# Inverse deviations on ScalarE, ranks behind the second transposition, and the first row loads from ScalarE's queue in a two-stage MetaFormer kernel

## The chip, the cores and the metric

One core of a Trainium2 chip. The time is the device time of one launch in microseconds (us), lower is better. "Profiled execution" is one run recorded by the hardware profiler; all rows and clock times below are of it, and its us count from the start of its span.

## The reference

The input `x` is 8 images of 64 channels and 16x16 pixels, so 2048 tokens of 64 channels.

```python
kq = w_kq @ xn + b_kq; v = w_v @ xn + b_v          # xn: layer norm of x over channels, eps 1e-6
ctx = softmax(kq.T @ kq) @ v                       # 256 x 256 per image
t = x + w_o @ ctx + b_o                            # a token is a row of 64
tn = layer_norm(t)                                 # eps 1e-5
probs = softmax(tn @ router_w.T)                   # 8 experts, the best 2 of each token
out = t + sum over the 2 chosen: gate * (silu(tn @ w1[e].T) * (tn @ w3[e].T)) @ w2[e].T   # 682 wide
```

All of it is fp32.

## The kernel before, in words

There is no scheduler: each engine runs its own hand-written instruction list, and semaphores tie the lists together. A wait holds back everything that stands behind it on its engine.

**Stage one** works on four pairs `p` of images, four tiles of 128 tokens each. Per pair, ScalarE normalises (`normalise`, L440), copies the transposed rows (`xT_copy`), the key-query product (`kq_copy`), the value product (`u_copy`) and the transposed weights (`probsT_copy`, L474), and takes `exponentials` (L466), two per pair. VectorE takes the row maxima (`row_max`), the sum of residual and attention (`residual`), the two best experts (`tops`, `choose`), and the moments of the new rows (`t_statistics`). TensorE's `rank(p)` counts, by matmuls of ones, how many tokens went to each expert before; from it VectorE makes the row number of each token (`positions`, L658 and L662), and `normalise_t` writes the normalised rows (`xrows`, L643). GpSimd scatters them to `xs` in HBM, sorted by expert: 8 indirect DMAs per pair, 32 in all (`scatter_row`, L374), one after the other. GpSimd also computes both inverse deviations, as variance plus epsilon to the power of -0.5 (`inverse_deviation`, `t_deviation`, L349 and L364), between its other work.

TensorE's list holds matmuls that compute nothing which is used (`fill`, `keep_busy`), between the others.

**Tables.** After pairs 0 and 1 (`KNOWN = (2, 3, 4)`), VectorE works out which expert each of the first 8 slots of 128 rows belongs to, and where its rows begin (`subtiles_of_experts`, `owners_of_slots`, `rows_of_slots`, L703). These are tables in SBUF; SyncE reads them into registers, one load per number (L298 the owner, L302 the row), and issues DMAs at those addresses: `load_weights(i)` four of 565 KB each per quad of slots (L294), `load_rows(i)` four of 32.5 KB (L310). Phase 1 opens slots 8 to 15 after pair 2, phase 2 slots 16 to 38 after pair 3. The row loads of a phase wait until its scatters have landed (`landed`).

**Stage two** has 39 slots in 10 quads. Per quad: VectorE doubles the loaded rows (`pair_up`, L791), TensorE turns them (`turn_x`, L1034), ScalarE copies them (`columns`, tile `x_cols`, L507). Then six steps of up projection (L1055, L1057), `silu` on ScalarE (L515), product on VectorE (`multiply`, tile `hid`, L836), and the down projection (L1082). `up(g)` waits for `multiply(g - 3)`, so TensorE can be three steps ahead of VectorE. VectorE's list puts `pair_up(i + 2)` ahead of the first `multiply` of quad `i + 1`, and puts table work between the multiplications of quads 0 and 1: `rows_of_slots(1)`, which ends with L714 and releases phase 1's loads, stands after the second product of quad 0, and the tables of phase 2 behind the last product of quad 1. GpSimd scatters the results to `ys` (L383). A last stage loads, weighs and adds them.

## Time and profile before

| | |
|---|---|
| median of 3 runs | 179.76 us (178.6 to 181.26) |
| profiled execution, its own time | 177.17 us |
| its span | 175.4 us |
| TensorE busy | 142.0 us (81%) |
| VectorE, GpSimd, ScalarE busy | 99.8, 85.8, 71.2 us |
| mean granted clock of TensorE | 0.942 of full speed |

The span is what the trace covers. Busy shares are means over stages with different limits, so they say little by themselves.

### The profile page before, as it was taken

To read this page: it belongs to the slowest core of one execution; us is meant where nothing else is said; L and a number is where in the kernel's file an instruction comes from. 1 tells how busy PE (TensorE), PEld (TensorE's weight loads), DVE (VectorE), ACT (ScalarE), POOL (GpSimd) and SP (SyncE) were. 2 spreads that over 40 slices of the span, in tenths; PEclk is the share of its full clock that TensorE was granted. 3 is DMA by queue.
4 is the path that set the end of the run, shared out by engine and by line. 5 is a ranking of instruction groups with operands and counts; after the bars stand their busy time and mean duration, and the time that the engine had idled before them with its cause. 6 is when DMAs were issued, how large, how long until landed. Compare 5 with 4: busy or idle time off the path is not lost.

```text
span 175.4 us, 4915 instructions
## 1 busy us (share of the span) xinstructions
PE 142.0 (81%) x1697; PEld 119.7 (68%) x1697; DVE 99.8 (57%) x372; ACT 71.2 (41%) x141; POOL 85.8 (49%) x114
## 2 busy tenths in 40 slices
PE   1489969590892596996699999999999999985672
PEld 1357746370561495895598999999999989874262
DVE  1626756858739857589357474637364736443050
ACT  2347664512430144262153545454545445443011
POOL 2695223877773772577653353525262626266000
PEclk9999999999579569999699999999999999999699
DMA  4999400001781692179697969596969881000345
GB/s 120 322 288 279 110 0 11 23 15 34 234 338 35 151 392 83 43 251 344 206 381 215 396 199 373 174 356 194 325 207 348 275 327 49 13 30 15 95 156 120
DMA packets 19893, 33.00 MB, mean 188 GB/s; under 512 B 7691, under 2 KB 13100, under 8 KB 19868
## 3 DMA queue, kind: packets, MB, share of 16 engines
q1 hardware_dynamic: 16732, 29.55, 52.1%
q0 software_dynamic: 2272, 2.35, 4.0%
q10 hardware_dynamic: 864, 0.79, 1.4%
q8 instruction: 14, 0.23, 0.6%
q14 instruction: 11, 0.09, 0.2%
HBM read 25.55 MB, written 7.13 MB: 186 GB/s over the span
## 4 chain that ended last, share of the span: by engine, by line
issue 31%; POOL 29%; PE 17%; DMA 8%; ACT 5%; DVE 5%; SPq 1%; POOLq 1%; ACTq 0%; DVEq 0%
POOL ys L383 20%; POOL xs L374 9%; PE psum L1055 4%; ACT probs L466 3%; DMA xs<-xrows,pos 2%; DMA y_in<-ys 2%; PE psum L1126 2%; PE psum L940 2%; PE psum L929 2%; PE psum L919 1%; DVE xrows L643 1%; DMA ys<-y_out,y_row 1%; DMA proj<-projections 1%; DMA x_in<-xs 1%; PE psum L1034 1%
## 5 line engine op out<-in xcount | busy, mean ns | idle before, releaser
L383 POOL DMA_INDIRECT ys<-y_out,y_row x39 | 37.7, 967 | 43.3 <-DVE y_out L848 34.1
L1055 PE MATMUL psum<-x_cols,weights 64*128 64x128 f32 x390 | 52.0, 288 | 3.5 <-DMA weights<-experts 3.3
L1055 PEld LDWEIGHTS psum<-x_cols,weights 64*128 64x128 f32 x390 | 48.1, 197 | 7.5 <-issue 5.4
L1057 PE MATMUL psum<-x_cols,weights 64*128 64x128 f32 x390 | 52.0, 288 | 0.0
L836 DVE TENSOR_TENSOR hid<-psum,act_sb 128x512 f32<-128x512 f32 (+1 forms) x50 | 33.7, 678 | 30.6 <-ACT act_sb L515 30.3
L1057 PEld LDWEIGHTS psum<-x_cols,weights 64*128 64x128 f32 x390 | 48.1, 197 | 0.0
L515 ACT ACTIVATE act_sb<-psum 128x512 f32<-128x512 f32 (+1 forms) x50 | 29.3, 586 | 29.8 <-PE psum L1055 29.8
L374 POOL DMA_INDIRECT xs<-xrows,pos x32 | 31.4, 980 | 18.4 <-DVE xrows L643 10.0
L1082 PE MATMUL psum<-hid,weights 128*64 128x128 f32 x468 | 28.8, 276 | 0.0
L1082 PEld LDWEIGHTS psum<-hid,weights 128*64 128x64 f32 x468 | 25.9, 137 | 1.8 <-DVE hid L836 0.3
L929 PE MATMUL psum<-ident,probs 128*128 128x128 f32 x32 | 6.6, 340 | 8.9 <-ACT probs L466 8.7
L929 PEld LDWEIGHTS psum<-ident,probs 128*128 128x128 f32 x32 | 4.2, 169 | 13.0 <-ACT probs L466 12.1
L528 ACT COPY y_cols<-psum 128x256 f32<-128x256 f32 (+1 forms) x10 | 3.6, 361 | 21.0 <-PE psum L1082 21.0
L507 ACT COPY x_cols<-psum 128x512 f32<-128x512 f32 (+1 forms) x10 | 5.7, 574 | 12.0 <-PE psum L1034 12.0
L1034 PE MATMUL psum<-ident,x_pairs 128*128 128x128 f32 x39 | 7.3, 316 | 3.0 <-DVE x_pairs L791 3.0
L940 PEld LDWEIGHTS psum<-u_sb,probsT 128*128 128x128 f32 x64 | 8.6, 209 | 1.0 <-issue 1.0
L940 PE MATMUL psum<-u_sb,probsT 128*128 128x73 f32 x64 | 9.3, 292 | 0.0
L981 PE MATMUL psum<-ones,before 128*128 128x512 bf16 x18 | 6.2, 488 | 3.5 <-issue 3.5
L466 ACT ACTIVATE probs<-psum,neg_max 128x256 f32<-128x256 f32 x16 | 6.7, 477 | 4.4 <-DVE neg_max L594 4.4
L1034 PEld LDWEIGHTS psum<-ident,x_pairs 128*128 128x128 f32 x39 | 4.7, 156 | 4.7 <-issue 2.3
L440 ACT ACTIVATE xn<-x_sb,shift_x,rstd 128x64 f32<-128x64 f32 x16 | 5.7, 429 | 5.2 <-DVE std L580 5.2
L839 DVE TENSOR_TENSOR hid<-psum,act_sb 42x512 f32<-42x512 f32 x10 | 6.8, 680 | 1.6 <-ACT act_sb L519 1.4
(150 smaller groups left out, 182.1 us busy)
## 6 DMA issues: line engine op xcount, KB each, us to landing
weights<-experts SPq DMA_DIRECT2D x39, 565.0 KB, 6.1
xs<-zeros SPq DMA_DIRECT2D x4, 1040.0 KB, 12.3
x_in<-xs SPq DMA_DIRECT2D x39, 32.5 KB
ys<-y_out,y_row POOLq DMA_INDIRECT x39
xs<-xrows,pos POOLq DMA_INDIRECT x32, 2.9
y_in<-ys ACTq DMA_DIRECT2D x2, 256.0 KB, 4.6
y_in<-ys SPq DMA_DIRECT2D x2, 256.0 KB, 4.3
x_sb<-x_tok SPq DMA_DIRECT2D x1, 384.0 KB, 3.6
```

The lines of the kernel that those rows point to most:

```text
L374: nc.gpsimd.indirect_dma_start(xs, bass.IndirectOffsetOnAxis(ap=pos[:, p, at:at + 1], axis=0), xrows[:, TPP * p + at // K_TOP, at % K_TOP, ...
L383: nc.gpsimd.indirect_dma_start(ys, bass.IndirectOffsetOnAxis(ap=y_row[:, j:j + 1], axis=0), y_out[:, i % RING, h, :], None).then_inc(y_sca ...
L466: ins = nc.scalar.activation(probs[:, b % 2, i, :], scores(b)[:, i, :], ACT.Exp, bias=neg_max[:, b, i:i + 1])
L515: nc.scalar.activation(live(i, act_sb[:, g % 3, :]), live(i, H1_BANK[g % 2]), ACT.Silu).then_inc(silu_done, 1)
L836: nc.vector.tensor_tensor(live(i, hid[:, i % 2, s, :]), live(i, H3_BANK[g % 3]), live(i, act_sb[:, g % 3, :]), ALU.mult).then_inc(hid_done, 1)
L839: nc.vector.tensor_tensor(hid[0:TAIL, i % 2, s, :].rearrange("p (k n) -> p k n", k=2), TAIL_BANKS[0:TAIL], act_sb[0:TAIL, g % 3, :].rearra ...
L929: ins = nc.tensor.transpose(PT_BANK[:, N * j + P * i:N * j + P * (i + 1)], probs[:, b % 2, i, P * j:P * (j + 1)], ident[:])
L940: ins = nc.tensor.matmul(O_BANK[b % 2][:, (TX + 1) * i:(TX + 1) * (i + 1)], probsT[:, b % 2, j, P * i:P * (i + 1)], u_sb[:, 2 * b + j, E:] ...
L1034: ins = nc.tensor.transpose(X_BANK[:, P * h:P * (h + 1)], x_pairs[:, i % 2, h, :, :], ident[:])
L1055: first_ = nc.tensor.matmul(H1_BANK[g % 2][:, src], weights[0:C, slot, P * s:P * (s + 1)], x_cols[0:C, i % 2, src], start=True, stop=True)
L1057: second_ = nc.tensor.matmul(H3_BANK[g % 3][:, src], weights[C:P, slot, P * s:P * (s + 1)], x_cols[C:P, i % 2, src], start=True, stop=True)
L1082: ins = nc.tensor.matmul(Y_BANK[C * (h % 2):C * (h % 2 + 1), P * (h // 2):P * (h // 2 + 1)], weights[:, slot, HP + C * s:HP + C * (s + 1)] ...
```

## The change

- Both inverse deviations go from GpSimd to ScalarE, as exp(-0.5 ln(variance + eps)). ScalarE's first table set holds both functions. Those of `x` are taken in two batches (4 tiles, then 12) instead of four; the other one is taken per pair inside ScalarE's loop, the last behind the first row loads.
- `fill(-1, 7)` and `fill(-1, 2)`: nine matmuls of 128x512 at the start; other counts of `fill` and `keep_busy` rise (10 in the third pass, 8 and 6 at the end). `ones` is set by VectorE.
- In the loop over pairs, both `exponentials` stand ahead of the first `probsT_copy`; `rank(p)` stands right behind `transpose_probs(2 * p + 3)`, ahead of `attend(2 * p + 2)` and the fills.
- The row loads of quads 0 and 1 are issued by ScalarE: it waits for the first table, loads 8 row numbers into registers, waits for the first 16 scatters, issues 8 DMAs, takes the last deviations, and loads the table for `silu`.
- SyncE issues the weights of quads 0 and 1 as soon as the first table is there. In phase 1 it issues the weights of quad 2 ahead of that quad's rows; before, rows came first.
- `pair_up(0)` stands behind `positions(3)` and `used_up(0)` on VectorE.

The diff, cut (`...` where lines are left out):

```diff
+        def batch(k):
+            return slice(TPP, TILES) if k else slice(0, TPP)
+
+        def scaled(p):
+            return 4 if p else 2
+
         def phase_of(p):
             return next(k for k in range(PHASES) if p < KNOWN[k])
...
+        def rows_of(engine, i):
+            return [engine.value_load(table[0:1, 1, QUAD * i + h:QUAD * i + h + 1], min_val=0, max_val=E * CAP - SUB)
+                    for h in members(i)]
+
+        def load_rows(engine, i, at):
+            if i >= XRING:
+                engine.wait_ge(y_row_ready, i - XRING + 1)
+                engine.wait_ge(x_paired, i - XRING + 1)
+            for h in members(i):
+                engine.dma_start(x_in[:, i % XRING, h, :], xs[bass.ds(at[h], SUB), :]).then_inc(x_in_loaded[i % XRING], 16)
+
+        def landed(engine, p):
+            engine.wait_ge(dispatched[p], 16 * TPP * K_TOP * (KNOWN[p] - (KNOWN[p - 1] if p else 0)))
...
             sp.wait_ge(table_ready, 1)
-            load_weights(0, owners_of(0))
-            early_rows, second_owners = [rows_of(0), rows_of(1)], owners_of(1)
-            landed(0)
-            load_rows(0, early_rows[0])
-            load_rows(1, early_rows[1])
-            load_weights(1, second_owners)
+            for i in quads_of(0):
+                load_weights(i, owners_of(i))
             for p in range(1, PHASES):
                 sp.wait_ge(table_ready, p + 1)
                 for i in quads_of(p):
-                    at = rows_of(i)
+                    if i < WQUADS:
+                        load_weights(i, owners_of(i))
+                for i in quads_of(p):
+                    at = rows_of(sp, i)
                     if i == quads_of(p)[0]:
-                        landed(p)
-                    load_rows(i, at)
-                    load_weights(i, owners_of(i))
+                        landed(sp, p)
+                    load_rows(sp, i, at)
+                    if i >= WQUADS:
+                        load_weights(i, owners_of(i))
...
-            def t_deviation(p):
-                pool.wait_ge(moments_t_ready, p + 1)
-                nc.gpsimd.tensor_scalar(variance_t[:, pair(p)], moments_t[:, pair(p), 1], EPS[1], None,
-                                        ALU.add).then_inc(variance_t_ready, 1)
-                pool.wait_ge(variance_t_ready, p + 1)
-                nc.gpsimd.tensor_tensor(rstd_t[:, pair(p)], variance_t[:, pair(p)], neg_half[:, pair(p)],
-                                        ALU.pow).then_inc(rstd_t_ready, 1)
...
-            t_deviation(0)
             for p in range(PAIRS):
                 for at in range(TPP * K_TOP):
-                    if p == 0 and at == TPP:
-                        t_deviation(1)
                     scatter_row(p, at)
-                if p == 1:
-                    t_deviation(2)
-                    t_deviation(3)
...
+            def inverse_deviations(k):
+                act.wait_ge(moments_ready, k + 1)
+                act.wait_ge(eps_set, 2)
+                nc.scalar.activation(logs[:, 0, batch(k)], moments[:, batch(k), 1], ACT.Ln, bias=eps[:, 0:1]
+                                     ).then_inc(logs_ready, 1)
+                act.wait_ge(logs_ready, k + 1)
+                nc.scalar.activation(rstd[:, batch(k)], logs[:, 0, batch(k)], ACT.Exp, scale=-0.5).then_inc(rstd_ready, 1)
+
+            def t_deviation(p):
+                act.wait_ge(moments_t_ready, p + 1)
+                nc.scalar.activation(logs[:, 1, pair(p)], moments_t[:, pair(p), 1], ACT.Ln, bias=eps[:, 1:2]
+                                     ).then_inc(logs_t_ready, 1)
+                act.wait_ge(logs_t_ready, p + 1)
+                nc.scalar.activation(rstd_t[:, pair(p)], logs[:, 1, pair(p)], ACT.Exp, scale=-0.5).then_inc(rstd_t_ready, 1)
+
             def normalise(p):
-                act.wait_ge(scale_ready, 2 * (p + 1))
+                act.wait_ge(scale_ready, scaled(p))
...
-            nc.scalar.preload_act_table(ACT.Exp)
+            nc.scalar.preload_act_table_set("natural_log_exp_and_others")
+            inverse_deviations(0)
             act.wait_ge(consts_loaded, 16 * CONST_DMAS)
             normalise(0)
             xT_copy(0)
             kq_copy(0)
+            inverse_deviations(1)
             normalise(1)
             exponentials(0)
             xT_copy(1)
@@ -491,13 +485,20 @@
                 if p + 2 < PAIRS:
                     normalise(p + 2)
                     xT_copy(p + 2)
+                exponentials(2 * p + 2)
                 u_copy(p + 1)
-                exponentials(2 * p + 2)
+                exponentials(2 * p + 3)
                 probsT_copy(2 * p + 2)
+                t_deviation(p)
                 if p + 2 < PAIRS:
                     kq_copy(p + 2)
-                exponentials(2 * p + 3)
                 probsT_copy(2 * p + 3)
+            act.wait_ge(table_ready, 1)
+            early_rows = [rows_of(act, i) for i in quads_of(0)]
+            landed(act, 0)
+            for i in quads_of(0):
+                load_rows(act, i, early_rows[i])
+            t_deviation(PAIRS - 1)
             nc.scalar.preload_act_table(ACT.Silu)
...
             x_statistics(0)
+            scales(0)
             dve.wait_ge(products_done, 1)
             nc.vector.tensor_copy(wuT[:], bank[7][0:C, 0:2 * P]).then_inc(products_copied, 1)
             nc.vector.tensor_copy(wr[:], bank[6][0:C, 0:E]).then_inc(products_copied, 1)
-            scales(0)
             dve.wait_ge(x_loaded[1], 16)
             x_statistics(1)
...
-                    pair_up(0)
                 positions(p)
                 if p < KNOWN[0]:
                     normalise_t(p)
             used_up(0)
+            pair_up(0)
...
+            fill(-1, 7)
...
+            fill(-1, 2)
             transpose_x(0)
             pe.wait_ge(products_copied, 2)
             nc.tensor.matmul(bank[6][:, E:2 * E], wuT[:, 0:P], wr[:], start=True, stop=True)
+            key_query(0)
             nc.tensor.matmul(bank[6][:, 2 * UW:2 * UW + E], wuT[:, P:2 * P], wr[:], start=True, stop=True
                              ).then_inc(bias_logits_done, 1)
-            key_query(0)
             similarity(0)
...
-                fill(p, 2)
+                fill(p, 2 if p < 2 else 10)
                 transpose_probs(2 * p + 2)
                 if p + 2 < PAIRS:
                     key_query(p + 2)
                 fill(p, 2)
                 transpose_probs(2 * p + 3)
+                rank(p)
                 attend(2 * p + 2)
-                fill(p, 3)
-                rank(p)
+                fill(p + 1, 2)
             attend(B - 1)
-            keep_busy(4)
+            keep_busy(8)
             rank(PAIRS - 1)
-            keep_busy(3)
+            keep_busy(6)
```

## Rows read from the trace of the kernel before

**Rows 1.** Busy time by stretch: from:to, us, busy (x) per engine, PEclk, DMA share, GB/s
```profile
78.00:87.00 9.00, 5.70 (x76) 4.98 (x73) 6.29 (x23) 1.92 (x4) 6.98 (x7) 0.88 0.83 274
...
96.00:105.00 9.00, 9.00 (x144) 8.40 (x146) 5.28 (x11) 4.56 (x9) 3.82 (x4) 1.00 0.83 301
```

**Rows 2.** ScalarE, first `silu` of quads 1, 3 and 4 in the timeline: start, us
```profile
73.57 0.60 ACT L515 ACTIVATE act_sb<-psum 128x512 f32<-128x512 f32 x1 [0.70 <-PE psum L1055]
...
97.03 0.60 ACT L515 ACTIVATE act_sb<-psum 128x512 f32<-128x512 f32 x1 [0.70 <-PE psum L1055]
...
106.00 0.60 ACT L515 ACTIVATE act_sb<-psum 128x512 f32<-128x512 f32 x1 [0.70 <-PE psum L1055]
```

**Rows 3.** Chain that ended last, 40 to 60 us: start, us, what
```profile
49.43 4.04 DMA xs<-xrows,pos
...
59.70 0.59 ACT x_cols L507
```

**Rows 4.** ScalarE timeline, 0 to 60 us: start, us, line, what, idle before
```profile
7.31 1.43 ACT L440 ACTIVATE xn<-x_sb,shift_x,rstd 128x64 f32<-128x64 f32 x4 [5.24 <-DVE std L580]
...
14.18 0.84 ACT L466 ACTIVATE probs<-psum,neg_max 128x256 f32<-128x256 f32 x2 [0.77 <-DVE neg_max L594]
...
24.17 0.84 ACT L466 ACTIVATE probs<-psum,neg_max 128x256 f32<-128x256 f32 x2
...
47.79 0.59 ACT L474 COPY probsT<-psum 128x512 f32<-128x512 f32 x1 [1.20 <-PE psum L929]
48.40 1.28 ACT L501 ACT_TABLE_LOAD   x1
```

**Rows 5.** TensorE timeline, 0 to 62 us: start, us, line, what
```profile
10.37 1.22 PE L900 MATMUL psum<-xT,proj 128*128 128x256 f32 x2
...
23.12 0.60 PE L900 MATMUL psum<-xT,proj 128*128 128x256 f32 x2
...
25.06 0.66 PE L929 MATMUL psum<-ident,probs 128*128 128x128 f32 x4 [0.92 <-ACT probs L466]
...
26.40 0.81 PE L974 MATMUL psum<-ones 128*128 128x512 bf16 x3
```

**Rows 6.** VectorE timeline, 0 to 62 us: start, us, line, what, idle before
```profile
24.58 0.19 DVE L589 TENSOR_TENSOR x_base<-x_base,bias_x 128x32 f32<-128x32 f32 x1
27.37 0.22 DVE L658 TENSOR_TENSOR place<-chosen,psum 128x64 f32<-128x64 f32 x1 [2.60 <-PE psum L964]
...
40.90 0.17 DVE L703 SCALAR_TENSOR_TENSOR table<-owner,row_at 128x8 int32<-128x8 f32 x1
```

**Rows 7.** GpSimd timeline, 0 to 60 us: start, us, line, what, idle before
```profile
28.76 1.22 POOL L374 DMA_INDIRECT xs<-xrows,pos  x1 [4.27 <-DVE xrows L643]
...
32.81 0.96 POOL L374 DMA_INDIRECT xs<-xrows,pos  x1 [0.30 <-issue]
...
35.40 1.10 POOL L374 DMA_INDIRECT xs<-xrows,pos  x1 [0.19 <-issue]
```

**Rows 8.** SyncE's queue, 41 to 90 us: start, us, line, what it issues
```profile
53.64 4.41 SPq L310 DMA_DIRECT2D x_in<-xs  x8
...
69.22 3.12 SPq L310 DMA_DIRECT2D x_in<-xs  x4
74.75 1.88 SPq L294 DMA_DIRECT2D weights<-experts  x4
79.07 2.48 SPq L310 DMA_DIRECT2D x_in<-xs  x4
```

**Rows 9.** VectorE timeline, 62 to 100 us: start, us, line, what, idle before
```profile
66.64 0.19 DVE L714 TENSOR_SCALAR table<-owned 128x8 int32<-128x8 f32 x1
...
73.81 0.43 DVE L791 COPY x_pairs<-x_in 128x512 f32<-128x512 f32 x1 [1.63 <-DMA x_in<-xs]
...
85.56 0.43 DVE L791 COPY x_pairs<-x_in 128x512 f32<-128x512 f32 x1 [1.23 <-DMA x_in<-xs]
```

**Rows 10.** TensorE timeline, 60 to 100 us: the first matmul of quad 2
```profile
85.02 0.55 PE L1055 MATMUL psum<-x_cols,weights 64*128 64x128 f32 x1 [3.30 <-DMA weights<-experts]
```

More of the change, by code:

```diff
@@ L110, in metaformer @@
         kq = sb("kq", [P, 2, N])
+        eps = sb("eps", [P, 2])
+        logs = sb("logs", [P, 2, TILES])
         u_sb = sb("u_sb", [P, TILES, UX])
@@ L753, in weigh @@
                                         ALU.mult).then_inc(gates_ready, 1)
+            nc.vector.memset(ones[:], 1.0).then_inc(ones_set, 1)
+            for k in range(2):
+                nc.vector.memset(eps[:, k:k + 1], EPS[k]).then_inc(eps_set, 1)
             nc.vector.memset(wu_x[:], 0.0).then_inc(rows_set, 1)
@@ L967, in fill @@
             def fill(p, n):
-                pe.wait_ge(ones_made, 2)
-                pe.wait_ge(probs_ready, 2)
+                pe.wait_ge(ones_set, 1)
+                if p >= 0:
+                    pe.wait_ge(probs_ready, 2)
                 if p >= 1:
```

69 lines of the change are left out of this document (19 added, 50 removed).

## The prediction

> **What bounds the kernel now.** I began with busy time by stretch. From 96 us on TensorE is busy in all of it at full clock [rows 1], and the first `silu` of one quad follows that of the quad before by 106.00 - 97.03 = 8.97 us [rows 2]. The change touches nothing there, so it can only move the start of that train, or what the train loses in its first quads. From 78 to 87 us TensorE is busy 5.70 of 9 us at a mean clock of 0.88 [rows 1]. The loss has a size: quads 1 and 2 took 97.03 - 73.57 = 23.46 us where 2 x 8.97 = 17.94 would do, so 5.5 us. Of that, 3.30 us is one wait, quad 2's first matmul for its weights [rows 10]; the rest is the half clock after it and the step before it.
>
> Then I read the chain backwards from `x_cols`, the last step ahead of quad 0's projections. The last of 16 scatters starts at 49.43 and lands 4.04 us later, at 53.47; then come row loads, `pair_up`, `turn_x`, and `x_cols` at 59.70 [rows 3]. Before 49.43 it is GpSimd alone: it starts at 28.76 and goes on scatter after scatter [rows 7]. So three things count: when the first scatter can start, how long 16 take, and what stands between their landing and `x_cols`. Last I read SyncE's queue and VectorE's waits for what it loads [rows 8, 9], because the change reorders that queue.
>
> **The change part by part.**
>
> *Start.* Before, `normalise(0)` waits until 7.31 for `std`, and the first `exponentials` start at 14.18, on the row maxima [rows 4]. The deviation now costs two short activations instead of two GpSimd steps. Two things work against it: seven fills ahead of the constant products (at the three in 0.81 us of [rows 5], 7 x 0.27 = 1.9 us at full clock, 3.8 us at half, which may delay the products a little), and statistics of 12 tiles that must be over before `normalise(1)`. For it: the same `key_query` took 1.22 us at 10.37 and 0.60 at 23.12 [rows 5], so TensorE runs at 1.2 GHz early and fills may raise it to 2.4. That work can't be priced from one row. It is worth nothing at least and the 2.0 us that four such halved steps give at most; I take 1.0, since `normalise(1)` on ScalarE, 1.43 us like the one at 7.31 [rows 4], now stands last ahead of the exponentials.
>
> *Ranks.* `place` waits 2.60 us for the rank, from the end of `x_base` at 24.77 to 27.37 [rows 6]. Before, the rank followed `attend` and three fills, which end at 26.40 + 0.81 = 27.21 [rows 5]; the transposition that `rank` will follow ended at 25.06 + 0.66 = 25.72 [rows 5]. So 27.21 - 25.72 = 1.5 us goes with the reordering on TensorE, and about 1.1 with the second exponentials, at 24.17 before [rows 4], moved ahead of two copies (0.59 us for the like of 47.79 [rows 4], the other somewhat less). That is the whole 2.6 us; VectorE is busy until 24.77, so more is not there. I take 2.5. `rstd_t` comes from ScalarE by then, where two small activations stand between copies; they delay the second `probsT_copy`, which `rank` doesn't need.
>
> *Scatters.* A second `t_deviation` on GpSimd stands between the fourth and fifth scatter: 35.40 - 32.81 = 2.59 us where one period is 0.96 + 0.30 = 1.26 [rows 7], so 1.33 us goes. Sum to the last landing: 1.0 + 2.5 + 1.3 = 4.8 us, at 48.6. Pair 1's positions move up with it and are no bound: GpSimd needs them 10 us after its first scatter.
>
> *Landing to `x_cols`.* Before, 59.70 - 53.47 = 6.23 us, set by the rows. Now two paths end there. Rows: the same 6.23 us, plus 0 to 1.2 for contention, as eight weight loads instead of four may be in flight; 48.6 + 6.2 + 0.6 = 55.4. ScalarE: eight issues (4.41 us on SyncE [rows 8]), two activations (0.6, from `rstd` of four columns being shorter than any row shown; between 0.3 and 1.0), and the table load of 1.28 us [rows 4]: 48.6 + 0.2 + 4.4 + 0.6 + 1.3 = 55.1. They tie. I take 55.4, a gain of 4.3 us. The 8 register loads on ScalarE start after its last `probsT_copy` (47.79 before [rows 4], some 42 now) and cost 0.6 us each, by SyncE's 2.4 us for four between the table (66.83) and its first row load (69.22) [rows 8, 9]; they end at 46.8, hidden by 1.8 us. If ScalarE comes later than 43.8, the excess is paid.
>
> The page "ScalarE: Activation LUTs" of the Trainium skill, section "What ACT_TABLE_LOAD costs", adds a drain of about 1380 ns to each table load. No row here shows one behind a load. By it ScalarE's path would end at 56.5 and the gain be 3.2 us.
>
> *Clock at quad 0.* More `keep_busy`, but TensorE then idles from about 48.5 to 53. Nothing for or against; the first quad stays as slow as it was.
>
> *Quad 2's weights ahead of its rows.* This removes the 3.30 us wait and what follows it, all of the 5.5 us. What is late next is those rows. The first table after the start is ready at 66.64 + 0.19 = 66.83, row loads are issued from 69.22, and `pair_up(2)` starts at 73.81, having waited 1.63 us for them already: 6.98 us after the table [rows 8, 9]. Now SyncE reads four owners (2.4 us), issues four weights, reads four row numbers, issues four row loads. This very sequence stands in the rows once: weights at 74.75, rows at 79.07, and `pair_up(3)` waits for them until 85.56, 10.8 us after the first weight issue [rows 8, 9]. So `pair_up(2)` starts 2.4 + 10.8 = 13.2 us after the table, 6.2 us later than before. The lower bound leaves the flying weights out: 2.4 + 1.9 + 2.4 + (73.81 - 69.22) = 11.3 us, 4.3 later. Queued behind it on VectorE is the first `multiply` of quad 1, and TensorE can be three steps ahead, of which about 1.0 us was slack. TensorE stands 3.3 to 5.2 us; I take 5.2, as the row with the weights in flight is the nearer. After a stop like that the clock fell (0.88 in [rows 1]); I put it at 1.5 us, between none and 3. Phase 2's tables on VectorE, hidden before under the wait for weights, show by 0.5. Together 7.2 us for the 5.5 removed: a loss of 1.7.
>
> In "DMA: Bandwidth & Descriptors" of the Trainium skill, section "Queues, rings and completion order", an engine consumes descriptors of one ring in order and takes turns between rings. By it the rows that SyncE issues behind its own weights must wait for them, and those from ScalarE's queue need not. The late `x_in` at 85.56 agrees for the first half; the second half no row here shows.
>
> **Sum.** -4.3 + 1.7 = -2.6 us on 177.17 us of the profiled execution, so 174.6; the median of the three runs stands 2.6 above that execution, and 179.76 - 2.6 = 177.2.
>
> **Rivals.**
>
> *Quad 2's rows don't hold anyone.* If the rows come by the lower bound and the clock stays up, the loss in quads 1 and 2 is 3.3 + 0.5 instead of 7.2: 177.2 - 3.4 = 173.8. If the phase 1 table also comes early, because quad 0 runs at 2.4 GHz, another 2 to 3 us go: 171. For it: more fills, and weights that start 5 us earlier. Against it: the table is released by a product of quad 0, whose place is not moved, and the queue's arithmetic.
>
> *The ranks don't come forward.* If `taken` or the copies hold the rank, only the start and the removed deviation are left, 2.3 us instead of 4.8: 177.2 + 2.5 = 179.7. Against it: VectorE has `taken` done before 24.58, and waits 2.60 us.
>
> *ScalarE's queue is the new bound.* Eight row issues stand ahead of `x_cols` in one engine's list. SyncE's mean was 4.41 / 8 = 0.55 us, but four took 3.12 us once [rows 8], 0.78 each. At twice SyncE's mean the path ends 4.4 us later, of which 0.3 is hidden: 181.3. At 0.55 + 0.83 us per issue it passes 183.4, slower than before by over 2%; at a triple, 8.8 - 0.3 more, 185.7. For it: no row shows a register-addressed DMA from ScalarE. Against it: nothing else is in that queue then.
>
> **How the numbers follow.** Forecast 0.46 (own range 175 to 179.5, from bounds of 3 to 5.3 us for the front and -1 to +2.5 for the quads); rows not late 0.32 (170.5 to 175); ranks not forward 0.10; ScalarE's queue 0.12 (180 to 186). Range 171.5 to 181.0. A measurement of this kernel tells about 2%, 3.6 us, from no change: faster than 176.2 takes the second case and a sixth of the first, 0.39; slower than 183.4 takes most of the last, 0.09; the rest, 0.52, is within 2%.
>
> **What the changed profile would show.** First exponentials at about 13.2; first scatter near 25.2, the sixteenth landed near 48.6, no idle gap between the fourth and fifth; `x_cols` near 55.4, released by ScalarE's own list or by `turn_x`. No wait for weights ahead of quad 2. Instead a wait of some 6 to 8 us of VectorE for `x_in` ahead of quad 1's products, TensorE idle about 5 us there, and a low clock after it. From quad 3 on 8.97 us per quad. I am wrong if that wait is under 3 us, if `x_cols` comes before 53 or after 58, or if the clock through quad 0 is another than before.

## The result, and the profile after

| | before | after |
|---|---|---|
| median | 179.11 us (20 runs) | 182.70 us (20 runs) |
| ratio | | 1.0252 [1.0203, 1.0302] |
| profiled execution, its own time | 177.17 us | 180.27 us |
| its span | 175.4 us | 178.5 us |
| mean granted clock of TensorE | 0.942 | 0.958 |

The change makes the kernel 2.5% slower. Ratios compare undisturbed runs only and medians take in all, so the two can differ by up to 1.5%.

Where it went can be read at six milestones of the two spans, in us:

| milestone | before | after | after less before |
|---|---|---|---|
| first scatter | 28.76 | 26.13 | -2.63 |
| `x_cols` of quad 0 | 59.70 | 58.07 | -1.63 |
| first `silu` of quad 1 | 73.57 | 71.34 | -2.23 |
| first `silu` of quad 3 | 97.03 | 98.29 | +1.26 |
| first `silu` of quad 9 | 150.52 | 153.14 | +2.62 |
| end of span | 175.4 | 178.5 | +3.1 |

Up to quad 1 the changed kernel is ahead. Quads 1 and 2 cost 3.49 us more than before, quads 3 to 8 another 1.36, the tail 0.48.

**The front.** ScalarE's timeline, then VectorE's, TensorE's and GpSimd's (start, us, line, what, idle before), of the kernel after:

```profile
5.14 0.30 ACT L415 ACTIVATE logs<-moments,eps 128x4 f32<-128x4 f32 x1 [3.05 <-DVE moments L574]
...
13.24 0.81 ACT L458 ACTIVATE probs<-psum,neg_max 128x256 f32<-128x256 f32 x2
```

```profile
23.61 0.20 DVE L629 TENSOR_TENSOR taken<-chosen 128x32 bf16<-128x32 f32 x1
...
24.39 0.19 DVE L590 TENSOR_TENSOR x_base<-x_base,bias_x 128x32 f32<-128x32 f32 x1
24.50 0.22 DVE L659 TENSOR_TENSOR place<-chosen,psum 128x64 f32<-128x64 f32 x1
```

```profile
8.94 1.22 PE L900 MATMUL psum<-xT,proj 128*128 128x256 f32 x2
...
23.95 0.18 PE L955 MATMUL psum<-taken,before 128*128 128x32 bf16 x1
```

```profile
26.13 1.16 POOL L363 DMA_INDIRECT xs<-xrows,pos  x1 [12.30 <-DVE xrows L644]
...
45.43 0.97 POOL L363 DMA_INDIRECT xs<-xrows,pos  x1 [0.30 <-issue]
```

The exponentials start 0.94 us earlier than in [rows 4]. The key-query product still takes 1.22 us, as in [rows 5]: the nine fills haven't made it faster. (The profile's clock column gives 1.00 there in both kernels; the slow pace shows in the product's time alone.) The wait ahead of `place` (2.60 us in [rows 6]) is gone whole. But `x_base`, the step ahead of it, ends at 24.58 where it ended at 24.77: VectorE's list came forward by 0.19 us and not by the 0.94 of the exponentials. Three lines of the kernel after show where the rest went, and two of the kernel before what they compare with:

```profile
11.91 1.43 ACT L432 ACTIVATE xn<-x_sb,shift_x,rstd 128x64 f32<-128x64 f32 x4 [0.80 <-DVE std L581]
13.39 0.69 PE L895 MATMUL psum<-ident,xn 128*128 128x128 f32 x2 [1.43 <-ACT xn L432]
18.34 0.17 DVE L601 RECIPROCAL inv_sum<-psum 128x2 f32<-128x2 f32 x1 [2.22 <-PE psum L940]
```

```profile
12.00 1.42 ACT L440 ACTIVATE xn<-x_sb,shift_x,rstd 128x64 f32<-128x64 f32 x4
18.54 0.17 DVE L600 RECIPROCAL inv_sum<-psum 128x2 f32<-128x2 f32 x1 [0.63 <-PE psum L940]
```

`normalise(1)` waits for a `std` that is now worked out for 12 tiles at once, and starts at 11.91, only 0.09 us earlier than before. TensorE's next transposition waits for it, and VectorE waits 2.22 us for the first `attend`, which ends 0.2 us earlier than before. The sixteen scatters take 19.30 us from first to last, against 20.67 in [rows 3, 7].

**From the scatters to `x_cols`.** The chain that ended last (start, us, what; a DMA's time runs from its issue to its landing), and ScalarE's timeline:

```profile
45.43 5.76 DMA xs<-xrows,pos
...
53.22 2.96 DMA x_in<-xs
...
56.27 0.44 DVE x_pairs L791
...
58.07 0.59 ACT x_cols L508
```

```profile
41.95 0.59 ACT L466 COPY probsT<-psum 128x512 f32<-128x512 f32 x1 [0.38 <-PE psum L929]
51.37 4.21 ACTq L279 DMA_DIRECT2D x_in<-xs  x8
55.63 0.30 ACT L422 ACTIVATE logs<-moments_t,eps 128x4 f32<-128x4 f32 x1 [13.09 <-issue]
55.96 0.20 ACT L425 ACTIVATE rstd_t<-logs 128x4 f32<-128x4 f32 x1
56.18 1.28 ACT L502 ACT_TABLE_LOAD   x1
58.07 0.59 ACT L508 COPY x_cols<-psum 128x512 f32<-128x512 f32 x1 [0.61 <-PE psum L1037]
```

Compare the first line with 49.43 and 4.04 us in [rows 3]: the last of the sixteen scatters is issued 4.00 us earlier, and takes 1.72 us longer to land. Busy time by stretch shows what else was moving (from:to, us, busy (x) of PE, PEld, DVE, ACT, POOL, PEclk, DMA share, GB/s), here with two stretches that are read below:

```profile
42.00:52.00 10.00, 5.98 (x52) 3.69 (x50) 6.97 (x46) 0.54 (x1) 6.27 (x7) 1.00 1.02 401
...
74.00:78.00 4.00, 0.00 (x0) 0.00 (x0) 0.59 (x3) 0.29 (x1) 3.08 (x4) 1.00 0.58 171
78.00:82.00 4.00, 3.35 (x32) 3.36 (x32) 3.17 (x10) 0.60 (x1) 2.93 (x4) 0.57 0.35 66
```

While the scatters finish, the DMA engines are busy all the time (a share of 1.02) at 401 GB/s; before, over the same stretch, it was 0.74 and 252. What is new there is eight weight loads of 565 KB where there were four. ScalarE's own list ends at 57.46, 0.61 us ahead of `x_cols`; the rows decide.

**Quads 1 and 2.** SyncE's queue, VectorE, TensorE, and the first `silu` of quads 2 to 5:

```profile
66.97 2.34 SPq L313 DMA_DIRECT2D weights<-experts  x4
71.74 6.18 SPq L279 DMA_DIRECT2D x_in<-xs  x8
80.33 1.96 SPq L313 DMA_DIRECT2D weights<-experts  x4
90.88 2.69 SPq L279 DMA_DIRECT2D x_in<-xs  x4
```

```profile
64.42 0.17 DVE L715 TENSOR_SCALAR table<-owned 128x8 int32<-128x8 f32 x1
...
77.41 0.43 DVE L791 COPY x_pairs<-x_in 128x512 f32<-128x512 f32 x1 [7.46 <-DMA x_in<-xs]
77.83 0.68 DVE L836 TENSOR_TENSOR hid<-psum,act_sb 128x512 f32<-128x512 f32 x1
...
88.26 0.18 DVE L715 TENSOR_SCALAR table<-owned 128x23 int32<-128x23 f32 x1
88.34 0.42 DVE L791 COPY x_pairs<-x_in 128x512 f32<-128x512 f32 x1
```

```profile
78.66 0.55 PE L1058 MATMUL psum<-x_cols,weights 64*128 64x128 f32 x1 [4.99 <-DVE hid L836]
...
88.82 0.66 PE L1037 MATMUL psum<-ident,x_pairs 128*128 128x128 f32 x4 [1.58 <-DVE x_pairs L791]
```

```profile
87.27 0.60 ACT L516 ACTIVATE act_sb<-psum 128x512 f32<-128x512 f32 x1 [0.70 <-PE psum L1058]
...
98.29 0.60 ACT L516 ACTIVATE act_sb<-psum 128x512 f32<-128x512 f32 x1 [0.70 <-PE psum L1058]
...
107.26 0.60 ACT L516 ACTIVATE act_sb<-psum 128x512 f32<-128x512 f32 x1 [0.70 <-PE psum L1058]
...
116.80 0.60 ACT L516 ACTIVATE act_sb<-psum 128x512 f32<-128x512 f32 x1 [1.28 <-PE psum L1058]
```

Read them in this order. The table is ready at 64.59, 2.2 us earlier than in [rows 9]. The weights are issued first, the rows from 71.74. `pair_up(2)` has waited 7.46 us when it starts, at 77.41, where [rows 9] have 1.63 us and 73.81. The products of quad 1 stand behind it, so TensorE waits 4.99 us for `hid`; after that idle stretch (74 to 78 us: nothing) its clock is 0.57 from 78 to 82. In exchange the wait of 3.30 us of [rows 10] is gone. Then `turn_x(3)` waits 1.58 us for a `pair_up` that stands behind phase 2's tables. Quad 1 took 87.27 - 71.34 = 15.93 us, quad 2 took 11.02.

The next quad takes 8.97 us, as in [rows 2], but the one after that takes 9.54: the train that ran evenly in the profile of before has gaps in its later quads here.

### The profile page after: what moved, and what is told of

Same layout as the page of the kernel before. It is cut to its first block, busy times and chain, and to the rows that moved or that the text cites. A ratio compares the mean times of both kernels' runs of the same rounds, so it can differ in the third digit from the quotient of the medians.

```text
span 178.5 us, 4955 instructions
## 1 busy us (share of the span) xinstructions
PE 146.0 (82%) x1718; PEld 119.7 (67%) x1718; DVE 98.3 (55%) x371; ACT 73.5 (41%) x153; POOL 75.5 (42%) x96
## 4 chain that ended last, share of the span: by engine, by line
issue 32%; POOL 28%; PE 15%; DVE 10%; DMA 9%; ACT 2%; ACTq 1%; POOLq 1%; DVEq 0%; SPq 0%
POOL ys L372 20%; POOL xs L363 8%; PE psum L1058 3%; DMA xs<-xrows,pos 3%; DMA y_in<-ys 2%; PE psum L975 2%; PE psum L1129 2%; DMA x_in<-xs 2%; DVE xrows L644 2%; DVE neg_max L595 1%; DMA ys<-y_out,y_row 1%; PE psum L900 1%; DVE rows L606 1%; PE psum L1037 1%; ACTq L279 1%
## 5 line engine op out<-in xcount | busy, mean ns | idle before, releaser
L791 DVE COPY x_pairs<-x_in 128x512 f32<-128x512 f32 (+1 forms) x10 | 4.4, 436 | 22.7 <-DMA x_in<-xs 22.7
L975 PE MATMUL psum<-ones 128*128 128x512 bf16 x35 | 11.3, 442 | 1.1 <-DVE ones L756 1.1
L982 PE MATMUL psum<-ones,before 128*128 128x512 bf16 x25 | 7.7, 456 | 3.5 <-issue 3.5
L940 PE MATMUL psum<-u_sb,probsT 128*128 128x73 f32 x64 | 8.6, 278 | 0.0
L940 PEld LDWEIGHTS psum<-u_sb,probsT 128*128 128x128 f32 x64 | 7.8, 191 | 1.1 <-issue 1.0
L929 PE MATMUL psum<-ident,probs 128*128 128x128 f32 x32 | 5.6, 302 | 2.8 <-ACT probs L458 1.7
## 6 DMA issues: line engine op xcount, KB each, us to landing
x_in<-xs SPq DMA_DIRECT2D x31, 32.5 KB, 3.8
```

What stands on the lines that cost most here:

```text
L929: ins = nc.tensor.transpose(PT_BANK[:, N * j + P * i:N * j + P * (i + 1)], probs[:, b % 2, i, P * j:P * (j + 1)], ident[:])
L940: ins = nc.tensor.matmul(O_BANK[b % 2][:, (TX + 1) * i:(TX + 1) * (i + 1)], probsT[:, b % 2, j, P * i:P * (i + 1)], u_sb[:, 2 * b + j, E:] ...
L975: nc.tensor.matmul(SPARE_BANK, ones[:], ones[:].unsqueeze(1).to_broadcast([P, BLK // P, P]), start=True, stop=True)
L982: nc.tensor.matmul(bank[4], before[:], ones[:].unsqueeze(1).to_broadcast([P, BLK // P, P]), start=True, stop=True)
```

## The experiments

Each ratio is to the kernel before, run beside it. Line numbers differ by a few between kernels.

**1. The order of SyncE's loads in phase 1, undone.** In the changed kernel, rows of each quad first, then its weights, as before:

```diff
-                for i in quads_of(p):
-                    if i < WQUADS:
-                        load_weights(i, owners_of(i))
...
                     load_rows(sp, i, at)
-                    if i >= WQUADS:
-                        load_weights(i, owners_of(i))
+                    load_weights(i, owners_of(i))
```

> The changed kernel with phase 1's queue in the old order: rows of quad 2, then its weights. Theory Q (the new order on SyncE makes the rows of quad 2 late, and that is dearer than the wait for weights it removes): pair_up(2) waits about 1.6 us instead of 7.5, the 3 us wait for weights ahead of quad 2 is back, quads 1 and 2 lose 5.5 us instead of 9.0, later quads get their weights in time again; 4 to 5 us faster than the changed kernel, so 0.985 to 0.995 of the kernel before. Rival S (the loss comes from the start or from ScalarE's queue): no faster than the changed kernel, ratio 1.02 or more.

Measured: 0.9861 [0.9751, 0.9972] of before. Nothing else is changed, and the kernel that was 2.5% slower than before is no longer slower. That it is faster is less sure: the interval nearly reaches 1, and the medians of all runs are 178.37 and 178.12 us. The chain, and TensorE's wait:

```profile
45.72 5.70 DMA xs<-xrows,pos
53.50 2.54 DMA x_in<-xs
```

```profile
82.57 0.34 PE L1054 MATMUL psum<-x_cols,weights 64*128 64x128 f32 x1 [2.60 <-DMA weights<-experts]
```

The wait for weights is back, and it is the cheaper one: quad 1 to quad 3 take 94.69 - 71.83 = 22.86 us instead of 26.95. Quads 3 to 8 run evenly here, in 53.49 us. The long landing stays.

**2. The second quad's weights, held until the scatters have landed.** The order of phase 1 is the changed kernel's.

```diff
-            for i in quads_of(0):
-                load_weights(i, owners_of(i))
+            load_weights(0, owners_of(0))
+            second_owners = owners_of(1)
+            landed(sp, 0)
+            load_weights(1, second_owners)
```

> The changed kernel, but SyncE issues the weights of quad 1 only after the first 16 scatters have landed, so four weight loads are in flight instead of eight. Theory W (the eight weight loads slow the last scatter's landing, 5.8 us instead of 4.0, and the first row loads): last landing 4.0 us after its start, x_in's landing 1.8 instead of 3.0 us after the fourth issue, x_cols 2.5 to 3 us earlier than at 58.1; total 2 to 3 us less than the changed kernel. Rival: the landing takes 5.8 us for another reason (position of the scatters, ScalarE's wait): x_cols within 0.5 us of 58.1. Counter-effect possible: quad 1 waits for its weights if they take over 10 us after the landing.

Measured: 1.0447 [1.032, 1.0574], slower than the kernel after and not faster as expected. The chain:

```profile
45.38 4.22 DMA xs<-xrows,pos
...
51.37 9.02 DMA x_in<-xs
...
62.28 0.59 ACT x_cols L510
```

The landing falls from 5.76 to 4.22 us, so the weights in flight did lengthen it. But now the four weight loads go out at the moment at which ScalarE issues its rows, and a row load takes 9.02 us. ScalarE's queue didn't protect these loads from SyncE's.

**3. Both edits together** (the two diffs above).

> Both edits on the changed kernel: old order in phase 1 and weights of quad 1 after the landing. If theories Q and W both hold and add, 6.5 to 8 us below the changed kernel, 0.965 to 0.98 of the kernel before. If they don't add, because an earlier quad 0 only makes the wait for quad 2's weights longer, about 0.985.

Measured: 1.024 [1.0169, 1.0312]; landing 3.75 us, row load 7.82, `x_cols` 60.94. Expected was 0.965 to 0.985. Against 2 the old order gives back 2% (3.5% by the medians), and the collision of 2 stays.

**4. The new order alone, in the kernel before.** Nothing of the change but this:

```diff
+                for i in quads_of(p):
+                    if i < WQUADS:
+                        load_weights(i, owners_of(i))
...
                     load_rows(i, at)
-                    load_weights(i, owners_of(i))
+                    if i >= WQUADS:
+                        load_weights(i, owners_of(i))
```

> The kernel before with one part of the change: in phase 1 the weights of quad 2 ahead of its rows. Theory Q: pair_up(2) starts about 13 us after the phase 1 table instead of 7.0, TensorE stands 5 us in quad 1, no wait for weights ahead of quad 2, quads 1 and 2 lose 9 us instead of 5.5, and SyncE's later weights come late by 1 us: 1.015 to 1.03 of the kernel before. Rival (an exchange of one wait for another): 0.99 to 1.01.

Measured: 1.0366 [1.0284, 1.0449], a little more than expected. VectorE and TensorE:

```profile
80.75 0.43 DVE L795 COPY x_pairs<-x_in 128x512 f32<-128x512 f32 x1 [7.52 <-DMA x_in<-xs]
```

```profile
82.00 0.55 PE L1059 MATMUL psum<-x_cols,weights 64*128 64x128 f32 x1 [5.06 <-DVE hid L840]
```

The same two waits as in the kernel after (7.46 and 4.99), and gaps later: quads 1 and 2 took 102.02 - 74.61 = 27.41 us, and quad 4 took 121.75 - 111.12 = 10.63. With 1 this shows the cause from both sides: this one reordering costs 3.7% put in (3.3% by the medians), and gives 3.8% taken out (0.9861 / 1.0252; 1.8% by the medians). The profiles agree. Quads 1 and 2 took 26.95 to 28.59 us in the four kernels with the new order (after, 2, 4 and 15), and 20.96 to 24.97 in the eleven with the old order whose list isn't otherwise changed (7, 10 and 12 left out).

**5. The second quad's weights behind the rows of quads 0 and 1**, on top of 1:

```diff
+            load_weights(0, owners_of(0))
+            second_owners = owners_of(1)
             for i in quads_of(0):
-                load_weights(i, owners_of(i))
+                sp.wait_ge(x_in_loaded[i], 16 * QUAD)
+            load_weights(1, second_owners)
```

> The changed kernel with phase 1 in the old order, and quad 1's weights issued only when the first eight row loads have landed. Theory R (row loads are slowed by weights in flight, whichever queue they are in): the last scatter lands in 3.8 to 4.3 us instead of 5.7, the rows 1.8 to 2 us after the fourth issue instead of 2.5 to 3, x_cols at 55.5 to 56.2 with ScalarE's list as the last to end (the same with weights behind the landing alone had 7.8 to 9.0 us for the rows). 2 us faster than the version with the old order alone, about 0.975 of the kernel before. Rival (the queue of its own protects the rows, the 7.8 us had another cause): x_cols as at 58, ratio 0.986 as without this edit.

Measured: 0.9919 [0.9858, 0.998] where 0.975 was expected; the medians are equal. The landing is 4.00 us and `x_pairs` comes 8.06 us after the sixteenth scatter instead of 10.41 in 1, but `x_cols` comes at 57.65. The chain now runs through ScalarE's list (its eight issues, the last deviations, the table load, which ends at 57.64): with the collision gone, ScalarE's own list is the bound, at 47.44 + 4.00 = 51.44 to 57.65, 6.21 us, which is no gain over the 6.23 of [rows 3].

**6. The first rows back on SyncE**, in the old order, with 1's order in phase 1. Of the change only the front before the loads is left. (Used again in 9 and 16.)

```diff
-            for i in quads_of(0):
-                load_weights(i, owners_of(i))
+            load_weights(0, owners_of(0))
+            early_rows, second_owners = [rows_of(sp, 0), rows_of(sp, 1)], owners_of(1)
+            landed(sp, 0)
+            load_rows(sp, 0, early_rows[0])
+            load_rows(sp, 1, early_rows[1])
+            load_weights(1, second_owners)
...
-            act.wait_ge(table_ready, 1)
-            early_rows = [rows_of(act, i) for i in quads_of(0)]
-            landed(act, 0)
-            for i in quads_of(0):
-                load_rows(act, i, early_rows[i])
```

> The changed kernel with all of the old order on SyncE: rows of quads 0 and 1 issued by SyncE, quad 1's weights behind them, phase 1 rows first. What is left of the change is the start, the deviations and the ranks. Theory F (these are worth 2.6 us at the first scatter and 1.3 us on GpSimd, 4 us at the landing): last landing 49.3 to 49.8 against 53.5 before. SyncE has read its 12 numbers by 45, so x_cols 6.2 us later at 55.8. 0.975 to 0.98 of the kernel before, and faster by 1 to 2 us than the version with rows on ScalarE and early weights. Rival (the start's gain is lost again later, since what follows is bound otherwise): 0.99 or more.

Measured: 0.9898 [0.985, 0.9946] where 0.975 to 0.98 was expected. The chain:

```profile
46.64 3.95 DMA xs<-xrows,pos
52.76 1.83 DMA x_in<-xs
...
56.03 0.59 ACT x_cols L503
```

Landing and row load are back at the values of [rows 3], and from landing to `x_cols` it takes 5.44 us. With those loads on ScalarE, 5 had 0.9919 beside it: moving them to ScalarE brought nothing that can be told. In this execution the last 32 matmuls took 5.47 us, in that of before 3.84, which led to 9.

**7. Owners announced before the rows' table**, on top of 1, so that quad 2's weights go out earlier without rows standing behind a table:

```diff
-                nc.vector.tensor_copy(table[:, 0, own], owner[:, own]).then_inc(dve_step, 1)
+                nc.vector.tensor_copy(table[:, 0, own], owner[:, own]).then_inc(owners_known, 1)
...
-                sp.wait_ge(table_ready, p + 1)
+                sp.wait_ge(owners_known, p + 1)
                 for i in quads_of(p):
                     if i < WQUADS:
                         load_weights(i, owners_of(i))
+                sp.wait_ge(table_ready, p + 1)
```

> The changed kernel with phase 1 in the old order, but quad 2's weights released by a signal of their own when its owners are known (about 59 us), not by the phase 1 table (65 us). They are issued and mostly landed before the rows. Theory Q says the two transfers only collide because one signal releases both: neither the 2.6 to 3.3 us wait for weights nor the 7.5 us wait for rows appears, quads 1 and 2 lose 1 to 3 us instead of 5.5 or 9; 3 to 4 us faster than with the old order alone, about 0.965 of the kernel before. Rival (the queue is slow whatever the order): rows of quad 2 late by 2 us or more behind these weights, ratio 0.98 or more.

Measured: 0.9923 [0.9871, 0.9974] where 0.965 was expected. The wait of TensorE for weights is gone, `pair_up(2)` waits 1.21 us only, and quad 1 takes 9.27 us. Then quad 2 takes 11.35, since `turn_x(3)` waits 1.92 us, and SyncE's rows are late in five later quads. No gain over 1 that can be told.

**8. More `keep_busy` ahead of `turn_x(0)`**, on top of 1: `keep_busy(30)` for `keep_busy(6)`.

> The changed kernel with phase 1 in the old order and 30 instead of 6 matmuls of keep_busy ahead of turn_x(0), so that TensorE idles 2 us instead of 7 before quad 0. If the half clock at the head of quad 0 costs what the rows suggest (first matmul to first silu 2.1 us at 1.2 GHz, 1.1 us at 2.4), quad 0 is 1 to 2 us shorter and the granted clock there 1.00; 0.98 of the kernel before. Rival (quad 0 is bound by VectorE's tables between its products): x_cols to the first silu of quad 1 stays 13.3 to 13.8 us, ratio as without it, 0.986.

Measured: 0.985 [0.9801, 0.9898] against 0.9861 in 1. From `x_cols` to quad 1's first `silu` 72.95 - 59.89 = 13.06 us; 13.80 in 1. That is 0.74 us less in the profile, but 6 and 9, which are the same kernel up to the tail, have 13.65 and 12.79 us there. So neither the ratio nor the profile shows a gain.

**9. Fills ahead of TensorE's last wait**, on top of 6:

```diff
+            keep_busy(20)
             all_scattered(pe)
             keep_busy(10)
```

> The version with all row loads back on SyncE in the old order, plus 20 matmuls of keep_busy in front of TensorE's last wait for the scatters. In that version quad 9 began 4.5 us earlier than in the kernel before, but the span was only 1.6 us shorter; its last 32 matmuls took 5.48 us instead of 3.85, at a lower clock, and the loads of the results 5.0 instead of 3.9. Theory C (part of the gain was lost to the half clock after the 5 us that TensorE waits there): last matmuls 3.85 us, 1 to 1.6 us faster than without, 0.975 to 0.98 of the kernel before. Rival (chance of one profile): no difference in the timed ratio, 0.985 to 0.99.

Measured: 0.9637 [0.9545, 0.9729], the fastest of all; the last matmuls took 3.84 us. Expected was 0.975 to 0.98. What this gain consists of is taken up in 13 to 16.

**10. Versions 7, 9 and more `keep_busy`** (14 for 6) together.

> All that helped together: start, deviations on ScalarE and ranks of the change; row loads of quads 0 and 1 on SyncE with quad 1's weights behind them; quad 2's weights released as soon as its owners are known; 14 matmuls ahead of turn_x(0); 20 in front of the last wait. If the parts add: x_cols at 56, no wait for weights ahead of quad 2 (quads 1 and 2 lose 3 us instead of 5.5), quad 0 shorter by 0.7, tail by 1: 0.96 to 0.965 of the kernel before. If SyncE's queue is the next bound (4 row numbers, 4 rows, 4 owners, 4 weights take 8.6 to 9.4 us per quad, TensorE 8.97), half of it is lost again: 0.975 to 0.98.

Measured: 0.9805 [0.9742, 0.9868]; the parts don't add, as the second of its expectations (0.975 to 0.98) had it. Quad 2 takes 93.08 - 80.03 = 13.05 us: the early owners give quad 1 its weights and take it back one quad on, as in 7.

**11. The reordered ranks alone, in the kernel before.**

```diff
-                u_copy(p + 1)
                 exponentials(2 * p + 2)
+                u_copy(p + 1)
+                exponentials(2 * p + 3)
                 probsT_copy(2 * p + 2)
...
-                exponentials(2 * p + 3)
...
-                attend(2 * p + 2)
-                fill(p, 3)
                 rank(p)
+                attend(2 * p + 2)
+                fill(p + 1, 2)
```

> The kernel before with only the new order in the loop over pairs: both exponentials ahead of the first probsT copy, rank behind the second transposition, fills behind it. Theory F: the rank part alone brings the first scatter forward by 1.7 to 2.5 us (28.8 to about 26.7), the last landing and x_cols by as much; 0.99 of the kernel before. Rival (the ranks' gain needs the earlier start and the deviations on ScalarE, since rstd_t or GpSimd's own work comes last): first scatter moves by under 0.5 us, ratio 1.00.

Measured: 0.9788 [0.9733, 0.9842], more than the 0.99 expected. First scatter 27.34 (1.42 us earlier), sixteenth 47.99, `x_cols` 57.73. This part alone is faster by about 2% of before, and TensorE waits 2.91 us for quad 2's weights, about as before.

The 1.42 us is less than the part is worth, because the profiles don't begin alike: VectorE's first statistics of `x` start at 4.05 us in before, at 4.10 in the kernel after and at 5.37 here.

```profile
4.05 0.59 DVE L570 BATCH_NORM_STATS2 parts<-x_sb 128x6 f32<-128x64 f32 x4
```

```profile
5.37 0.59 DVE L570 BATCH_NORM_STATS2 parts<-x_sb 128x6 f32<-128x64 f32 x4
```

From there to the first scatter it takes 24.65 to 25.01 us in the four profiles with the front of before (before, 4, 12, 13), 21.97 and 22.23 in the two with the ranks alone (11, 14), and 21.69 to 23.09 in the twelve with the whole front. So the reordered ranks bring 2.5 to 2.7 us beside the 24.71 of before, and the rest of the front adds nothing to it.

**12. Two unused register loads more per quad on SyncE in phase 2, in the kernel before.**

```diff
                     load_rows(i, at)
+                    if p == PHASES - 1:
+                        for h in range(2):
+                            sp.value_load(table[0:1, 1, QUAD * i + h:QUAD * i + h + 1], min_val=0, max_val=E * CAP - SUB)
                     load_weights(i, owners_of(i))
```

> The kernel before with two more register loads per quad in SyncE's list in phase 2 (six quads), whose values are not used: 1.2 us more per quad for an engine that computes nothing. Theory S (SyncE's own list, some 8.7 us per quad, is nearly as long as TensorE's 8.97, so that late starts in phase 2 are never caught up): quads 5 to 9 take 9.7 to 9.9 us each in place of 8.97, 3 to 5 us slower, 1.015 to 1.03 of the kernel before. Rival (SyncE has slack, late weights had another cause): quads stay at 8.97 us, ratio 1.00.

Measured: 1.0305 [1.0231, 1.0379], at the upper end of what was expected. First `silu` of quads 5, 6, 7 and 8:

```profile
116.67 0.60 ACT L518 ACTIVATE act_sb<-psum 128x512 f32<-128x512 f32 x1 [0.70 <-PE psum L1058]
126.12 0.60 ACT L518 ACTIVATE act_sb<-psum 128x512 f32<-128x512 f32 x1 [1.18 <-PE psum L1058]
135.86 0.60 ACT L518 ACTIVATE act_sb<-psum 128x512 f32<-128x512 f32 x1 [0.97 <-PE psum L1058]
146.98 0.60 ACT L518 ACTIVATE act_sb<-psum 128x512 f32<-128x512 f32 x1 [1.64 <-PE psum L1058]
```

Quads now take 9.45, 9.74 and 11.12 us. SyncE's list per quad, from 1's queue (rows from 86.50 for 1.89, weights from 90.80 for 1.92, rows again at 95.53): two sets of four issues, 3.8 us, and two gaps of at least 2.4 us for four register loads each, so 8.6 us at least, against 8.97 for TensorE's quad. With 0.4 us of slack per quad, a queue that enters phase 2 late catches up slowly. How late it is shows in how far its first row loads of phase 2 are issued ahead of quad 3's first `silu`. Leaving out 12 itself, in the eight profiles in which that is 8.0 us or more (before: 97.03 - 88.87 = 8.16), quads 3 to 8 took 53.5 to 53.6 us. In nine it is 6.6 to 7.7 (the kernel after: 98.29 - 90.88 = 7.41); eight of these took 54.5 to 55.8 us, four of them with phase 1's rows first (5, 8, 9 and 11), and 15 is the exception, with 7.41 like the kernel after but 53.51 us. So a late queue goes with the gaps, but the new order is neither needed for them nor sure to bring them.

**13 to 16. The tail's fills, taken apart**, four kernels side by side. 13 is the kernel before with 9's fills, 14 is 11 with them, 15 the changed kernel with them, 16 is 9 again.

> The kernel before with 20 fills ahead of TensorE's wait for the last scatter to y, and nothing else. If those fills only keep the clock up: at most 1.6 us less than before (5.48 - 3.85 us for the last 32 matmuls), ratio 0.990 to 1.0; the profiled execution of before had its low stretch in the tail at 163.3 to 166.7 us, so most of it may not be there to gain. If the clock of the tail doesn't depend on them: 1.0.

> Ranks behind the second transposition as the only part of the change, with the same 20 fills in the tail. If the reordered ranks are what the change has of gain in front: ratio 0.965 to 0.975, as the kernel with the whole front, the old order of the loads and these fills (0.9637). If logarithm and exponential and the early constants are worth something besides: 0.975 or more.

> The changed kernel with the 20 fills in the tail alone. Its order of loads is what costs: ratio 1.01 to 1.02, since the fills can give at most 1.6 us (0.009) back of the 1.025. If it comes to 1.0 or less, the slower tail and not the order of the loads was the cause.

> The kernel with all of the change but the new order and queue of the loads, and the 20 fills, beside the three others on one chip: 0.96 to 0.97 as before. Against ranks alone with the fills: 1.0 us less (first exponentials 0.94 us earlier) if the front's other parts add up with ranks, 0 if they don't.

| | ratio to before | median, us |
|---|---|---|
| 13, before with tail fills | 1.0086 [1.0043, 1.013] | 179.31 |
| 14, ranks alone with tail fills | 0.9763 [0.9658, 0.9867] | 175.26 |
| 15, after with tail fills | 1.0231 [1.0159, 1.0303] | 180.77 |
| 16, as 9 | 0.979 [0.9738, 0.9843] | 173.52 |

13 missed its expectation: the fills give before nothing, and cost it a little. 15 stays slower than before, a little over what was expected: the fills don't mend the changed kernel. 16 came to 0.979 where the same kernel had 0.9637 as 9 (by the medians of all runs 0.974 and 0.973), so two measurements of one kernel can stand 1.5% apart in the ratio, and a difference of that size is read only between kernels that ran side by side (1 to 4, 5 to 8, 9 to 12, 13 to 16), and with care even there. 14 and 16 can't be told apart by their ratios. The landing of 16 took 3.57 us, its row load 2.02.

The profiles show why the fills pay after 6 and not in before. From quad 9's first `silu` to the end it takes 27.77 us in 6, and 24.97 and 25.04 in 9 and 16; in before it was 24.88 already, and 25.45 in 13. Fills can give back only a slow tail, and the profiled execution of before had none.

## Why the prediction was wrong, point by point

It forecast 177.2 us in a range of 171.5 to 181.0, a gain of 2.6; the time was 182.7, a loss of 3.6. Only its third rival, ScalarE's queue, reaches that time (180 to 186), and its mechanism didn't occur: the eight issues took 4.21 us, 0.53 each. The steps that failed are terms of the sum. The gain at the start was counted and didn't reach the first scatter; the landing was carried over unchanged; the loss behind the new order of the loads was taken as 1.7 us; and nothing was allowed for the quads from 3 on.

- **Start**: 1.0 us for the exponentials, measured 0.94. Right for them, but worth nothing at the first scatter. The prediction named the reason, statistics of 12 tiles ahead of `normalise(1)`, and gave it no price: `normalise(1)` starts 0.09 us earlier than before, and TensorE and VectorE wait for what follows from it.
- **Ranks**: 2.5 us. The wait of 2.60 us went whole, and ranks alone bring 2.5 to 2.7 us, counted from the first statistics (11 and 14). But the sum added Start to it, and VectorE's own list, which was named as the limit ("busy until 24.77"), came forward by 0.19 us only. First scatter at 26.13 instead of 25.2; the two terms together were 2.63 us instead of 3.5.
- **Scatters**: 1.33 us for the removed GpSimd step, measured 1.37.
- **Landing to `x_cols`**: this step failed by size. The landing itself was carried over at 4.04 us, and contention was allowed only for the way after it, 0.6 us. Measured: 1.72 us more for the landing, and 0.65 more from landing to `x_cols`, together 2.37. With eight weight loads in flight the landing took 5.70, 5.76, 5.86, 5.87 and 6.10 us in five kernels; with four it took 3.35 to 5.03 in all others whose chain was read. The rest of the way was right, 0.65 us for 0.6. So `x_cols` gained 1.63 us instead of 4.3. ScalarE's side of the tie was priced well: 6.27 us from the landing to the end of the table load, 6.5 by its terms.
- **Clock at quad 0**: nothing forecast. From `x_cols` to quad 1's first `silu` it took 13.27 us instead of 13.87, a gain of 0.60. TensorE's granted clock was 0.68 from 60 to 62 us and 1.00 from there; before, it was 0.50 from 60 to 64. The gain is no larger than the scatter between 6 and 9.
- **Quad 2's weights ahead of its rows**: right in mechanism and place, too small in price. `pair_up(2)` 12.8 us after the table (13.2 forecast), TensorE's wait 4.99 (5.2), half clock after it. The loss of quads 1 and 2 grew by 3.49 us and not by 1.7: phase 2's tables don't show by 0.5 us but hold `pair_up(3)`, for which `turn_x(3)` waits 1.58 us. That is 1.1 of the 1.8 us missed. Beside its wait quad 1 lost 15.93 - 8.97 - 4.99 = 1.97 us, where 1.5 was put down, and quad 2 lost 11.02 - 8.97 - 1.58 = 0.47, where nothing was. Experiments 1 and 4 show that the order alone makes the difference between slower and not slower.
- **From quad 3 on**: "8.97 us per quad" was wrong for this profile, by 1.36 us. Not in the working at all was SyncE's list, nearly as long as TensorE's quad; 12 shows how near the two are. Nor does this loss come in every execution: 15 has the same order and the same 7.41 us, and no gaps, and four kernels with phase 1's rows first have gaps.
- **The tail**: 0.48 us. The loads of the results took 4.32 us instead of 3.86, which is nearly all of it. In 15 they took 3.90 and in 13, without the change, 4.38, so it is scatter between executions and not the change, as far as these profiles show.

By these: -1.63 - 0.60 + 3.49 + 1.36 + 0.48 = +3.1 us, the measured difference of the spans, where the forecast had -2.6.

Rows behind SyncE's own weights waited, as the prediction read "DMA: Bandwidth & Descriptors" of the Trainium skill (section "Queues, rings and completion order"). It also concluded that rows of another queue need not wait; 2 shows 9.02 us for them. The table load's drain of about 1380 ns, from "ScalarE: Activation LUTs" of the Trainium skill (section "What ACT_TABLE_LOAD costs"), would, if it stood behind the load, put `x_cols` no earlier than an estimated 57.46 + 1.38 = 58.84. It started at 58.07, and in 5 it started at 57.65, right behind a load that ended at 57.64. Nor did it stand ahead of the load, which starts at 56.18, 0.02 us after the activation before it. No drain of that size is in these traces.

Open: whether logarithm and exponential on ScalarE and the constants at the start are worth anything in the time besides the ranks. They bring nothing at the first scatter, but the GpSimd step that they remove is 1.3 us of the sixteen scatters (19.31 us in 16, 20.66 in 14). The ratios of 14 and 16 overlap. The best that was measured is the kernel of 9 and 16, 0.9637 and 0.979, and it beats both kernels.

## What to carry to other kernels

Before you issue a transfer earlier, look at what is in flight at its new time: here small loads and the landing of indirect scatters, which sit on the chain, paid for large ones that don't, on either of the two queues. When a step starts earlier, follow it down to the next meeting point before you add its gain to another's: the start's 0.94 us was gone at the first scatter. When two loads of one queue change places, price the second as late by the first's whole flight, and then follow who is queued behind its consumer. And add up the issuing engine's own list per turn of the loop: at 8.6 of 8.97 us it takes part in the race, and a delay at the entry is made up slowly if at all.

## What the runs showed of the hardware

- A row load of 32.5 KB (the last of quad 0's four), issued by ScalarE while four loads of 565 KB had just gone out from SyncE, took 7.82 and 9.02 us (3 and 2). With eight such loads issued some 10 us earlier it took 2.54 to 3.77 (1, 7, 8, 15 and after), with four 1.70 to 2.56, then issued by SyncE.
- An indirect scatter's landing went from 3.35 to 5.03 us up to 5.70 to 6.10 when eight such loads instead of four were in flight.
- A register load on SyncE cost 0.6 us (gaps of 2.4 us for four), a DMA issue 0.47 to 0.91 (1.88 to 3.64 us for four), on ScalarE 0.53 (4.21 us for eight): a loop of eight of each was at least 8.6 us of SyncE's list.
- A table load on ScalarE took 1.28 us, with no more than 0.03 us between it and the activation ahead of it (after, 5), and 0.01 us to the one behind it where that had nothing else to wait for (5).
- One kernel measured twice gave 0.9637 and 0.979 of the same kernel before; from the first work on `x` to the first scatter it was 21.69 and 21.97 us.
